# Expert blocks that prepare the next segment: the high parts of the normalised rows move from VectorE to ScalarE, and VectorE's low parts move one group later

## The reference

```python
x = x + 0.5 * _L0_ffn_ref(_layernorm(x), gate_w, expert_bias, w1, w2)
x = x + _L0_attn_ref(_layernorm(x), ...)            # 16 heads of 8, banded prior added to the scores
x = x + 0.5 * _L0_ffn_ref(_layernorm(x), gate_w, expert_bias, w1, w2)

# _L0_ffn_ref
logits = einsum('btd,ed->bte', x, gate_w) + expert_bias      # 12 experts, 4 of them pass x through
topk_logits, topk_idx = top_k(logits, 2)
topk_w = softmax(topk_logits)
h = silu(einsum('btd,efd->btef', x, w1))                     # 8 experts, 128 -> 256 -> 128
y = einsum('btef,edf->bted', h, w2)
out = einsum('bte,bted->btd', w_ffn, y) + w_zero * x
```

## Time and profile before

| what | us |
|---|---|
| median of 3 runs (lowest, highest) | 1061.54 (1059.39, 1062.21) |
| the profiled execution: its own time | 1060.38 |
| span in its trace | 1058.6 |
| PE busy | 902.3 |
| DVE busy | 881.0 |
| ACT busy | 690.6 |
| POOL busy | 592.9 |

### The profile page before, as it was taken

The page is one execution under the profiler, slowest core; times in us unless marked ns, Lnnn a source line. Parts: engine busy times, 40 slices in busy tenths (PEclk is TensorE's granted clock), DMA queues, the critical chain, the costliest instruction groups (busy, mean ns, idle before and its releaser), DMA issues.

```text
span 1058.6 us, 36550 instructions
## 1 busy us (share of the span) xinstructions
PE 902.3 (85%) x13644; PEld 620.3 (59%) x13644; DVE 881.0 (83%) x2323; ACT 690.6 (65%) x1341; POOL 592.9 (56%) x666
## 2 busy tenths in 40 slices
PE   3276778898989999999888999998989999895785
PEld 3166644457855555555786555556865558643674
DVE  6977747799779999999977999999769888884687
ACT  2171674567788666666777866667788668774574
POOL 6570375762026566664302777774135776777776
PEclk9895977899999999999999999999999999998898
DMA  8601455655534342223462222326662247815564
GB/s 265 206 29 31 100 150 140 186 110 104 130 94 137 109 133 77 69 67 90 91 144 87 74 75 74 85 67 115 150 154 67 64 100 154 187 39 119 124 165 108
DMA packets 202698, 118.38 MB, mean 112 GB/s; under 512 B 98560, under 2 KB 193375, under 8 KB 202272
## 3 DMA queue, kind: packets, MB, share of 16 engines
q1 hardware_dynamic: 187424, 89.40, 33.5%
q0 software_dynamic: 15104, 26.65, 10.0%
HBM read 35.07 MB, written 64.26 MB: 94 GB/s over the span
## 4 chain that ended last, share of the span: by engine, by line
PE 46%; DVE 29%; issue 10%; ACT 8%; POOL 3%; DMA 2%; SPq 1%; DVEq 0%; POOLq 0%; ACTq 0%
DVE row_max L1615 7%; PE banks L715 7%; PE banks L744 7%; PE banks L690 5%; DVE h_lo L1500 4%; PE banks L506 3%; ACT probs L1010 3%; PE banks L599 2%; POOL big L1104 2%; PE banks L601 2%; PE banks L756 2%; PE banks L602 2%; PE banks L560 2%; DVE stats L1283 2%; PE banks L562 2%
## 5 line engine op out<-in xcount | busy, mean ns | idle before, releaser
L1010 ACT ACTIVATE probs<-banks 128x512 f32<-128x512 f32 x512 | 278.2, 597 | 140.2 <-PE banks L715 137.9
L1615 DVE TENSOR_REDUCE row_max<-banks 128x2 f32<-128x512 f32 x512 | 334.1, 684 | 23.6 <-PE banks L715 18.2
L1104 POOL DMA_INDIRECT big<-yg,slots x236 | 236.5, 1002 | 207.9 <-issue 111.6
L1090 POOL DMA_INDIRECT xg<-xs,slots x236 | 235.4, 998 | 138.5 <-issue 63.2
L599 PE MATMUL banks<-w_all,h_hi 128*128 (+1 forms) x800 | 150.9, 222 | 54.8 <-DVE h_lo L1500 53.5
L744 PE MATMUL banks<-probs,v_op 128*32 128x256 f32 x2048 | 180.5, 384 | 5.0 <-ACT ot_sb L1003 2.6
L1500 DVE TENSOR_TENSOR h_lo<-h_f,h_hi 128x512 bf16<-128x512 f32 x200 | 135.4, 687 | 53.6 <-ACT h_hi L924 50.0
L922 ACT ACTIVATE h_f<-banks 128x512 f32<-128x512 f32 x200 | 120.2, 601 | 85.2 <-PE banks L562 81.5
L715 PE MATMUL banks<-band_parts,thirds 96*32 96x296 bf16 (+2 forms) x4096 | 174.1, 277 | 0.0
L601 PE MATMUL banks<-w_all,h_hi 128*128 (+1 forms) x800 | 147.2, 222 | 0.1
L602 PE MATMUL banks<-w_all,h_lo 128*128 (+1 forms) x800 | 146.6, 221 | 0.0
(11 more groups left out here) (188 smaller groups left out, 1680.7 us busy)
## 6 DMA issues: line engine op xcount, KB each, us to landing
yg<-y_rows SPq DMA_DIRECT2D x77, 256.0 KB
q_in<-kq_kept SPq DMA_DIRECT2D x96, 64.0 KB
k_op<-kq_kept SPq DMA_DIRECT2D x96, 64.0 KB
xg<-zeros SPq DMA_DIRECT2D x5, 896.0 KB
kq_kept<-kq_hi SPq DMA_DIRECT2D x32, 128.0 KB
kq_kept<-kq_lo SPq DMA_DIRECT2D x32, 128.0 KB
xg<-zeros SPq DMA_DIRECT2D x1, 3968.0 KB, 14.1
xg<-zeros SPq DMA_DIRECT2D x2, 1984.0 KB
```

What stands on the lines that cost most here:

```text
L1010: act.activation(probs[:, four % 2, u % 4, :], banks[:, ST[u % 2], :], ACT.Exp).then_inc(A["exp_done"], 1)
L1090: pool.indirect_dma_start(xg[q], bass.IndirectOffsetOnAxis(slots[:, q % 4, c, t:t + 1], 0), xs[:, NTH[q] % 2, t, :], None, bounds_check=CA ...
L1104: pool.indirect_dma_start(y_back[:, i, c, :], None, yg[q], bass.IndirectOffsetOnAxis(slots[:, q % 4, c, t:t + 1], 0)).then_inc(gathered[i] ...
L1615: dve.tensor_reduce(row_max[:, gp, :, qt, j], banks[:, MX[(16 * b + v) % 3], :].rearrange("p (k c) -> p k c", k=2), AX.X, ALU.max).then_in ...
```

## The change

In the four blocks, the cast of a chunk is no longer made by DVE in `token_split` but by ACT in the new `high_rows`, at the same group 4 + 2k. There it stands in ACT's queue behind the group's two silu activations (and, in an even group, ahead of the copy `turn`, since `high` comes before `turn` in `plan`), and it waits for `xn_ready` of its chunk and for scatters that ended long before. DVE's subtraction becomes `low_rows`, at group 5 + 2k, behind the `rows` of chunk k + 1 that stand at the same group, and it waits for ACT's cast. Sizes, buffers and all other entries of `plan` stay. It concerns 6 + 7 + 5 + 3 = 21 chunks.

```diff
-              "rows": [3 + 2 * k for k in range(nk)], "split": [4 + 2 * k for k in range(nk)],
+              "rows": [3 + 2 * k for k in range(nk)], "high": [4 + 2 * k for k in range(nk)],
+              "split": [5 + 2 * k for k in range(nk)],
               "turn": [6 + 2 * k for k in range(nk)], "gate": [7 + 2 * k for k in range(nk)],
...
+            def high_rows(q, k):
+                act.wait_ge(scattered[NTH[q] % 2], landed(ROUTED[NTH[q] - 2]))
+                act.wait_ge(R["xn_ready"], K0[q] + k + 1)
+                t0, t1 = chunk(q, k)
+                r0 = (OFF[q] + t0) % XB
+                act.activation(xs[:, NTH[q] % 2, t0:t1, 0:D], xn[:, r0:r0 + t1 - t0, :],
+                               ACT.Copy).then_inc(R["hi_done"], 1)
...
                     for what, i in at.get(g, ()):
+                        if what == "high":
+                            high_rows(nxt, i)
                         if what == "turn":
                             token_cols(nxt, i)
...
+            def low_rows(q, k):
+                dve.wait_ge(R["hi_done"], KB[q] + k + 1)
+                t0, t1 = chunk(q, k)
+                r0 = (OFF[q] + t0) % XB
+                dve.tensor_tensor(xs[:, NTH[q] % 2, t0:t1, D:2 * D], xn[:, r0:r0 + t1 - t0, :],
+                                  xs[:, NTH[q] % 2, t0:t1, 0:D], ALU.subtract).then_inc(R["split_done"], 1)
...
                         if what == "split":
-                            token_split(nxt, i)
+                            low_rows(nxt, i)
```

## The result

The changed kernel is slower: median 1068.73 us of five runs (1067.57 to 1071.56) against 1061.54 (1059.26 to 1063.42), a ratio of 1.0076 with a 95% interval of 1.0058 to 1.0094. The forecast of 1063.8 and its range up to 1066.8 were too low. The profiled execution took 1067.57, with a span of 1065.8, 7.2 us over the span of before.

A forecast was written before the change was run, and what follows sets the result against it. DVE was taken to bound a block's front, PE its middle. Later `gate` 0 in blocks 1 to 4 summed to 1.25 + 0.2 + 0.3 + 0.6 = 2.35 us, giving 1063.8 us against the median 1061.5; range 1060 to 1066.8.

The forecast's parts named there:

- so I give the clock no part in the sum: Blocks' front and middle: PE's granted clock was 1.00 even where PE had gaps, so it was given no cost.
- the forecast's wait: Block 1, before `gate` 0: PE waits some 2.5 us, with ACT's `xt_f` as the releaser.
- The queue order: Block fronts: copies ahead of silu 5 and `xt_f` 0 delay `gate` 0; cost 1.25, 0.2, 0.3, 0.6 us in blocks 1 to 4.
- The middle of the blocks: Middle groups: the copy takes 0.49 of ACT's 0.61 us idle per two groups, so it costs nothing there.
- The slower rival: Middle of blocks: from a 0.72 us copy on, ACT bounds and every `gate` waits; 5.6 us more, 1067.1; chance 0.25.
- the rule that the prediction cited: ACT's queue is strictly first in, first out, so ready work stays behind a waiting copy; then 2.4 us more.
- The gain rival: Block fronts: PE does not come to wait for the copy, DVE's saving stands; 2.4 us less, 1059.1; chance 0.15.

The follow-up runs named there:

- e2: Changed kernel plus 34 unused matmuls on PE just ahead of `gate` 0 in blocks 1 and 2: median 1064.69 us, ratio 1.0025 to the kernel before.
- e1: Changed kernel with `xt_f` of the turned chunk ahead of the new copy in ACT's queue: median 1059.99 us, ratio 0.9984 to the kernel before.
- e4: Changed kernel with ACT's copy and DVE's subtraction both one group later (5 + 2k, 6 + 2k): median 1059.92 us, ratio 0.9977 to the kernel before.
- e6: Changed kernel with copy and subtraction of chunk 1 alone one group later (7 and 8): median 1061.0 us, ratio 0.9989 to the kernel before.
- e7: Changed kernel with ACT's copy at 5 + 2k and DVE's subtraction at 7 + 2k: median 1057.08 us, ratio 0.9957 to the kernel before.
- e5: Kernel before plus one PE wait for the rows of chunk 1 before `gate` 0 of blocks 1 to 4: median 1065.76 us, ratio 1.0032.
- e3: Kernel before with only DVE's subtraction one group later (5 + 2k), the cast staying on DVE: median 1059.9 us, ratio 0.9991.
- e0: The changed kernel itself measured again, nothing else altered: median 1068.86 us, ratio 1.0057 to the kernel before.

## Why the prediction was wrong

**The step that failed** is the one at the end of its first part: "so I give the clock no part in the sum". It rested on rows in which PE had gaps and the clock stayed at 1.00; the gap read in them was 0.64 us, while the sum itself put a wait of some 2.5 us in one place. The last part named a clock below 1.00 as a cost that the sum lacked; it had neither a chance nor a price. In the change PE's wait is followed by the lower level in three blocks of four, in both profiled executions, and e2, which takes the lower level away and leaves the wait, is faster by 4.2 us by the medians; in the profiles blocks 1 and 2 lose 4.5 us less (1.76 instead of 6.25).

The trace of before could have given a bound. In its four blocks PE's longest waits, all at 1.00, were these; behind the blocks, a wait of 5.82 us that ended at 982.28 stands in a stretch at the lower level:

```profile
555.58 0.32 PE L516 MATMUL banks<-chosen,tri_h 128*128 128x336 bf16 x1 [1.59 <-DVE chosen L1351]
...
567.28 0.23 PE L599 MATMUL banks<-w_all,h_hi 128*128 x1 [1.68 <-DVE h_lo L1500]
```

```profile
981.00:992.00 11.00, 9.71 (x62) 8.74 (x63) 6.60 (x17) 4.51 (x9) 8.46 (x9) 0.53 0.32 56
```

So the full clock was on record there for waits up to 1.68 us, and the forecast's wait was longer than any of them.

**The queue order was right, and a little larger than worked out.** `gate` 0 came later by 2.21, 2.21, 0.49 and 0.75 us (its start after, less its start before, less the block's own shift in the table), where the working had 2.04, 2.04, 0.29 and 0.57. Part of the difference is the copy: it takes 0.63 instead of 0.60 and holds the queue for 0.53 or 0.54 instead of 0.49. Carried through the same sums that makes 1.4, 0.4, 0.5 and 0.75 instead of 1.25, 0.2, 0.3 and 0.6, some 3.0 us instead of 2.35. For blocks 1 and 2 that is 1.8, and e2, which has the wait without the lower clock, lost 1.76 in them. What remains of the table, 8.9 less 3.0, is 5.9 us. That the clock is all of it is shown for blocks 1 and 2 alone; in size it has room for it: the windows of the blocks lose 3% of 66.5, 5% of 70.5 and 3% of 67.3 us, about 7.5, not all of it where PE sets the pace. Block 4, where the clock did not fall, lost 0.61 and had been given 0.6.

**The middle of the blocks** costs nothing, as said: ACT's idle time per two groups goes from 0.61 to 0.40 us, `gate` waits for no later chunk, the clock is at 1.00. The slower rival, with a time near the one measured, is thus not what happened: its place was this middle, and the copy's 0.63 is below its 0.72; that its time came nearer is luck. e1, e4 and e6, all with 21 copies, say the same.

**The queue** of ACT does hold ready work behind a waiting copy: 2.63 and 1.82 us in the rows above, `up` 5 long done and the transposes of chunk 0 too. Here the trace agrees with the rule that the prediction cited from the Trainium skill, "TensorE: Matmul & The Clock Gate", section "Architectural detail: the array is 16× 32×32, not 1× 128×128"; e1 shows its price, since it changes nothing but the order.

**The gain rival** had the saving right and the place wrong. It needs the copy where the rows are already there: e4 and e7 have it, 2.1 and 4.8 us under before by their medians, and it was worked out as 2.4. (e7 also takes the subtraction out of the way, which the rival left in place.)

**The range** was made from two rivals that were each one mechanism of the queues. A consequence of the forecast's own step, a PE that stands still for 2 us, was outside it, so its upper end fell short by 1.9 us.

**Open.** The four waits over 2 us in these blocks (blocks 1 and 2 of the change, in two executions) were all followed by the lower level, but below that the length of a wait does not decide. It followed 0.76 us in block 3 of the change and 1.37 in e5, but not 1.47 in e5, 1.21 in e6, 0.60 in block 4, nor 0.79 in block 3 of e2, which stands behind nearly the same waits as in the change (1.49 us before a `down`; 1.43 there). Late in block 2 all ten profiled executions have PE wait 1.58 or 1.59 us and then 1.68 to 1.77. The level fell behind both in e1, e3 and e5, behind the second in e4, and behind neither in the other six, the kernel before and the change among them. Outside these blocks the kernel before keeps 1.00 behind waits of 2.40 and 2.77 us, at 112.54 and 118.85. What else decides was not settled. And the 1.5 us that the change got back behind block 4 (2.2 in e0) were not followed up; there the clock moves between its levels in every execution.

## What to carry to other kernels

Moving work to an engine with spare time puts it into that engine's queue at a place: ask what it waits for there and what stands behind it, and put it where its input is already old. A new wait on PE that is longer than those which the trace has at the full clock should be priced twice, as the wait and, with a chance, as matmuls at half the clock behind it; in blocks 1 and 2 the second was 4.5 us and the first 1.8. One group more of distance between producer and consumer turned a loss of 0.6 to 0.8% into a gain of 0.2% with the same instructions (e4), and a second group for the subtraction made it 0.4% (e7).

## What was not expected of the hardware

A wait of 2.06 us on PE, between stretches at the full level, was followed after about 1.8 us by some 3 us at 0.50; the same wait of another execution (2.15) was followed by over 6. 34 unused matmuls in the wait, at two places, kept the level at 1.00 there and made the kernel 4.2 us faster by the medians. Waits of 1.59 to 1.77 us late in block 2 were followed by the lower level in some executions and by the full one in others. The SBUF-to-SBUF copy of 128x512 from f32 to bf16 takes 0.63 us on ACT, about as long as one from PSUM (0.60), while DVE's cast took 0.42.
